# Blocks turned by TensorE's transpose instead of an fp32 matmul with the identity, in two stages of a fused convolution, attention and expert kernel

## The chip, the cores and the metric

The kernel runs as one program on one core of a Trainium2 chip. Its time is the device time of one execution in microseconds (us). The kernel before takes 1914.7 us, the median of three runs (1913.49 to 1919.65).

## What is computed

The input is x, 128 images of 256 channels and 9 x 9 pixels, in fp32. Cut to what bears on the change:

```
xn  = layernorm of x over the channels                      # per image and pixel
k1  = 9-tap convolution of xn along the channels, one filter for each of the 81 pixels, + bias
v   = 3x3 depthwise convolution of xn (one filter per channel) + bias
k1s = relu(batchnorm(3x3 depthwise convolution of xn))
out1, out2 = two attentions made of xn, k1, v and k1s
x   = x + alpha * out1 + (1 - alpha) * out2
t   = x as 10368 tokens of 256 channels
t   = t + mixture of 8 experts (two chosen per token) of layernorm(t)
```

The two stages in which the change lies make k1 ("the pixel convolution") and then v and k1s ("the depthwise convolutions").

## The kernel before, in words

The core's engines run five instruction streams that are tied by semaphores. The order on each engine is written out by hand.

**Pixel stage.** 81 pixels are taken in 27 turns of three. ScalarE normalises the three pixels of a turn out of `big` into `xp_s` (L1207; image on the partitions, 256 channels along the row). TensorE turns each of the six 128 x 128 blocks, so that channels lie on the partitions (`turn_pixels`, L408, to PSUM). ScalarE copies the turned blocks to `xt_s` (L1214). TensorE convolves them with banded matrices, two fp32 matmuls of 132 columns per pixel (`convolve_pixels`, L419 and L421). VectorE adds the bias and writes k1 to `pool_` (L770), and it copies the normalised pixels back to `big` (L763). Everything is double-buffered, and TensorE turns the blocks of turn i+1 ahead of the convolution of turn i.

**Depthwise stage.** 256 channels go in 8 chunks of 32, and each chunk in 8 quads of four channels. A chunk begins with the turning of its first quad. Then TensorE makes the chunk's convolution matrices, nine times nine small bf16 matmuls (L457), which ScalarE (L1242, five times) and VectorE (L820, four times) copy to `m_s`; the PSUM banks for it are two pairs, so each group of nine matmuls waits for the copy two groups back. Then come the quads. For each, GpSimd copies four channels of xn (L1397), TensorE turns the four 128 x 81 blocks (`turn_quad`, L441), VectorE copies the result to `pt_s` (L826), TensorE multiplies it with the four channels' matrices (L475, 162 columns), ScalarE copies the two results out (L1251, L1253) and SyncE stores them. TensorE's order is: turn of quad q+1, then the multiplication of quad q. Before the first multiplication of a chunk it waits for the last copy of the matrices (L1242).

TensorE's other turned blocks, those of the attention (L531), of the token rows (L592), of the expert rows (L637) and of the end (L695), already go through `nc.tensor.transpose`.

A matmul with fp32 operands shows as two pairs of records in the trace, each a weight load (LDWEIGHTS, engine PEld) and a MATMUL (engine PE). So the 6 blocks of a pixel turn are 12 records at L408, and the 4 blocks of a quad are 8 records at L441.

Of the kernel before, what the change touches and what calls it, by code (L numbers as in the profile page):

```python
# [4 lines left out]
BS, C, H, W = 128, 256, 9, 9  # L5
HW = H * W
# [39 lines left out]
def metaformer_kernel(nc, x, taps, tap_bn, tap_rows, toeplitz_mask, ident, band_masks, rot_masks, zstrings,  # L46
# [14 lines left out]
    with ctx:  # L61
        def sb(name, shape, dt=fp32):
            return ctx.enter_context(nc.sbuf_tensor(name, shape, dt))
# [15 lines left out]
        ident_s = sb("ident_s", [128, 128])  # L79
# [42 lines left out]
        def take_aux(parts, *dims, dt=fp32):  # L122
            n = 1
            for d in dims:
                n *= d
            words = n if dt != fp16 else n // 2
            a = aux[0:parts, aux_at[0]:aux_at[0] + words]
            aux_at[0] += words
            assert aux_at[0] <= AUX
            a = a if dt == fp32 else a.bitcast(dt)  # L130
            names = "abcde"[:len(dims)]
            if len(dims) > 1:
                a = a.rearrange(f"p ({' '.join(names)}) -> p {' '.join(names)}",
                                **{m: d for m, d in zip(names, dims)})
            return a
# [3 lines left out]
        xp_s = take_aux(128, 2, PIX, C)  # L139
# [3 lines left out]
        ps = ctx.enter_context(nc.psum_tensor("ps", [128, 8, 512], fp32))  # L143
# [17 lines left out]
        xq_s = take_aux(128, 2, QUAD, HW)  # L161
# [235 lines left out]
        def _(pe):  # L397
            pe.wait_ge(S["w_in"], W_IN)

            def turn_pixels(i, par):  # L400

                pe.wait_ge(S["xp_c"], i + 1)
                pe.wait_ge(S["xt_c"], i - 1 + CREDIT)
                for k in range(PIX):
                    for h in range(HALVES):
                        at = (k % 2) * C + h * 128

                        last = nc.tensor.matmul(ps[:, 2 * par + k // 2, at:at + 128], xp_s[:, par, k, h * 128:(h + 1) * 128],  # L408
                                                ident_s[:, :], start=True, stop=True)
                last.then_inc(S["tr_c"], 1)  # L410

            def convolve_pixels(i, par, come):
# [10 lines left out]
                last.then_inc(S["k1_c"], 1)  # L423

            turn_pixels(0, 0)
            with pe.Fori(0, PIX_TURNS // 2) as i:
                for par in range(2):
                    turn_pixels(i * 2 + par + 1, 1 - par)
                    convolve_pixels(i * 2 + par, par, i + 1)
# [5 lines left out]
            def turn_quad(q, par):  # L435

                pe.wait_ge(S["xq_c"], q + 1)
                pe.wait_ge(S["pt_c"], q - 1 + CREDIT)
                for c in range(QUAD):

                    last = nc.tensor.matmul(ps[0:HW, 4 + par, c * BS:(c + 1) * BS], xq_s[:, par, c, :],  # L441
                                            ident_s[:, :], start=True, stop=True)
                last.then_inc(S["tq_p"], 1)

            per_chunk = CHUNK // QUAD
            with pe.Fori(0, C // CHUNK) as i:
                turn_quad(i * per_chunk, 0)

                pe.wait_ge(S["ks_c"], i * per_chunk + CREDIT)
                pe.wait_ge(S["tapc_c"], i + 1)  # L450
                for n in range(9):
# [4 lines left out]
                    for m in range(9):  # L456
                        last = nc.tensor.matmul(flat[:, m * 2 * CHUNK:(m + 1) * 2 * CHUNK].rearrange("p (v c) -> p v c", v=2),  # L457
                                                mask_s[:, n * 9 + m, :],
                                                tapc_s[:, :, :],
                                                start=True, stop=True)  # L460
                    last.then_inc(S["mb_p"], 1)
                for k in range(per_chunk):
                    q, par = i * per_chunk + k, k % 2
                    if k + 1 < per_chunk:
                        turn_quad(q + 1, 1 - par)
                    if k == 0:
                        pe.wait_ge(S["mb_e0"], i * 5 + 5)
                        pe.wait_ge(S["mb_e1"], i * 4 + 4)
                    pe.wait_ge(S["pt_c"], q + 1 + CREDIT)
                    if k >= 2:  # L470
                        pe.wait_ge(S["ks_c"], q - 1 + CREDIT)
                    b0 = 6 if par == 0 else 2
                    for c in range(QUAD):
                        o = ps[:, b0 + c // 2, (c % 2) * 2 * HW:(c % 2 + 1) * 2 * HW]
                        last = nc.tensor.matmul(o, pt_s[:, par, c, :], m_s[:, k * QUAD + c, :, :]  # L475
                                                .rearrange("p v n -> p (v n)"), start=True, stop=True)
                    last.then_inc(S["cv_p"], 1)
# [3 lines left out]
            for h in range(HALVES):  # L481
                last = nc.tensor.matmul(ps[:, 6, 0:EXPERTS], ones_s[:, :], router_s[:, h, :], start=h == 0, stop=h == 1)
# [207 lines left out]
            with pe.Fori(0, TURNS) as g:  # L690
                pe.wait_ge(S["mix_c"], g + 1)
                pe.wait_ge(S["fin_c"], g + CREDIT)
                for h in range(HALVES):
                    for s in range(SUBS):
                        last = nc.tensor.transpose(ps[:, h, s * 128:(s + 1) * 128], mix_s[:, s, h * 128:(h + 1) * 128],  # L695
                                                   ident_s[0:128, 0:128])
# [849 lines left out]
```

## Time and profile before

| what | value |
|---|---|
| median of three runs | 1914.7 us |
| profiled execution: span from the first to the last instruction | 1986.5 us |
| TensorE matmul busy in the span | 1444.1 us (73%) |
| mean granted TensorE clock | 0.817 of full |
| pixel stage | about 67 to 151 us of the span |
| depthwise stage, TensorE | 175 to 396 us of the span |
| L408: records, busy | 324, 44.6 us |
| L441: records, busy | 512, 78.9 us |

The page gives no other time for the profiled execution than its span; the span is 71.8 us above the median of the runs. The granted clock is a share of full speed: 1.00 is 2.4 GHz and 0.50 is 1.2 GHz. "PE" is the matmul side of TensorE, "PEld" its weight loads, "DVE" VectorE, "ACT" ScalarE, "POOL" GpSimd and "SP" SyncE. Matmuls are pipelined, so the busy time of a single record (some 275 ns at full clock) is longer than the step from one record to the next (some 110 ns).

### The profile page before, as it was taken

Reading aid. Unit: us, or ns where it says so; the run is one execution under the profiler, and the core shown is the slowest. Engines: PE = TensorE matmul, PEld = TensorE weight load, DVE = VectorE, ACT = ScalarE, POOL = GpSimd, SP = SyncE. Lnnn points to the kernel's source line nnn. Section 1 sums busy time; section 2 is a strip of 40 time slices with the busy share of each in tenths; the row PEclk is TensorE's granted clock in tenths of the full one; section 3 lists DMA queues with packets and bytes.
Section 4 is the critical chain, followed back from the end, with each engine's and each line's share of the span. In section 5 each row is a group of like instructions: output and inputs, shape, how many; then the busy total and the mean of one; then the engine's idle time right before and its main releaser. Section 6 shows DMA issues by size and latency. Waiting matters only on the chain.

```text
span 1986.5 us, 37743 instructions
## 1 busy us (share of the span) xinstructions
PE 1444.1 (73%) x10088; PEld 1176.6 (59%) x10089; DVE 1129.8 (57%) x2738; ACT 733.0 (37%) x1671; POOL 523.6 (26%) x520
## 2 busy tenths in 40 slices
PE   0594888889999999985454526999999999811111
PEld 0594888846666666655343425888888888711111
DVE  6893333356667666746666665555555555434443
ACT  0692444444444344426555542333333333200000
POOL 0000111124333333314555550000000000077764
PEclk9996788889999999965555557999999999955555
DMA  8424445476766676612222233222222222246655
GB/s 285 102 72 169 173 182 187 159 189 164 171 165 156 152 182 153 158 38 94 96 94 97 96 124 109 90 84 95 85 90 90 88 91 84 69 118 140 141 126 117
DMA packets 312390, 251.93 MB, mean 127 GB/s; under 512 B 184061, under 2 KB 290894, under 8 KB 311652
## 3 DMA queue, kind: packets, MB, share of 16 engines
q1 hardware_dynamic: 292719, 198.56, 35.1%
q0 software_dynamic: 19648, 53.11, 9.6%
q8 instruction: 9, 0.15, 0.0%
q14 instruction: 14, 0.11, 0.0%
HBM read 151.84 MB, written 105.39 MB: 129 GB/s over the span
## 4 chain that ended last, share of the span: by engine, by line
PE 60%; DVE 14%; issue 9%; POOL 7%; DMA 3%; ACT 3%; another core or an unknown queue 2%; DVEq 1%; SPq 1%; ACTq 0%; POOLq 0%
PE ps L668 12%; PE ps L653 11%; POOL aux L1444 7%; PE ps L492 5%; PE ps L475 4%; PE ps L441 3%; PE ps L519 3%; PE ps L547 2%; PE ps L543 2%; ACT pool_ L1242 2%; PE ps L502 2%; PE ps L637 2%; PE ps L511 2%; PE ps L545 2%
## 5 line engine op out<-in xcount | busy, mean ns | idle before, releaser
L1444 POOL DMA_INDIRECT aux<-y_d,idx_s x162 | 172.5, 1065 | 602.8 <-issue 595.7
L668 PE MATMUL ps<-pool_,aux 128*128 x2112 | 248.6, 274 | 10.8 <-DVE aux L1128 4.4
L653 PE MATMUL ps<-aux,pool_ 128*128 128x256 f16 x2112 | 246.6, 274 | 0.4 <-DVE aux L1120 0.4
L668 PEld LDWEIGHTS ps<-pool_,aux 128*128 128x128 f16 x2112 | 199.2, 98 | 56.6 <-issue 31.5
L653 PEld LDWEIGHTS ps<-aux,pool_ 128*128 x2112 | 207.3, 98 | 24.6 <-issue 0.8
L1421 POOL DMA_INDIRECT rows_d<-aux,idx_s x162 | 157.7, 974 | 168.5 <-issue 101.0
L1134 DVE SCALAR_TENSOR_TENSOR pool_<-ps,pool_ 128x512 f32<-128x512 f32 x88 | 60.9, 692 | 243.8 <-PE ps L668 243.8
L1365 ACT ACTIVATE aux<-ps,b_s 128x256 f32<-128x256 f32 x352 | 137.8, 474 | 160.5 <-DVE aux L1128 160.5
L695 PE MATMUL ps<-ident_s,aux 128*128 128x128 f32 x162 | 41.5, 429 | 201.2 <-DVE aux L1173 139.8
L695 PEld LDWEIGHTS ps<-ident_s,aux 128*128 128x128 f32 x162 | 30.8, 221 | 211.9 <-issue 211.9
L1397 POOL COPY aux<-big 128x324 f32 x64 | 29.2, 457 | 360.9 <-PE ps L441 186.9
L492 PE MATMUL ps<-pool_,se_w_s 81*81 81x512 f32 x256 | 118.7, 607 | 5.7 <-DMA pool_<-k_d 5.7
L1413 POOL DMA_DIRECT2D pool_<-v_d x64 | 50.0, 781 | 274.2 <-PE ps L549 269.5
L1357 ACT ACTIVATE aux<-ps 128x512 f16<-128x512 f32 x88 | 52.6, 597 | 181.7 <-PE ps L637 181.7
L1128 DVE TENSOR_TENSOR aux<-aux 128x1024 f16<-128x1024 f32 x88 | 107.8, 1225 | 3.1
L1277 ACT ACTIVATE pool_<-ps,sa_ab 128x324 f32<-128x324 f32 x64 | 39.7, 620 | 159.4 <-PE ps L504 159.4
L441 PE MATMUL ps<-ident_s,aux 128*81 128x128 f32 x512 | 78.9, 305 | 25.4 <-POOL aux L1397 25.4
L610 PE MATMUL ps<-aux,before_s 128*128 128x8 f32 x54 | 16.1, 372 | 110.8 <-DVE aux L1032 89.9
L408 PE MATMUL ps<-ident_s,aux 128*128 128x128 f32 x324 | 44.6, 290 | 69.6 <-ACT aux L1207 69.6
L826 DVE COPY aux<-ps 81x512 f32<-81x512 f32 x64 | 43.9, 686 | 87.7 <-PE ps L441 87.7
L1289 ACT ACTIVATE pool_<-ps,pool_ 128x81 f32<-128x81 f32 x256 | 79.5, 336 | 29.4 <-DVE pool_ L857 29.4
L475 PE MATMUL ps<-pool_,aux 82*128 82x162 f32 x512 | 89.7, 324 | 0.0
(203 smaller groups left out, 3111.9 us busy)
## 6 DMA issues: line engine op xcount, KB each, us to landing
pool_<-rows_d SPq DMA_DIRECT2D x88, 256.0 KB, 2.7
y_d<-pool_ SPq DMA_DIRECT2D x88, 256.0 KB, 2.2
big<-in_x SPq DMA_DIRECT2D x2, 5184.0 KB, 20.8
xn_d<-big SPq DMA_DIRECT2D x16, 648.0 KB, 3.0
v_d<-aux SPq DMA_DIRECT2D x64, 162.0 KB, 1.9
ks_d<-aux SPq DMA_DIRECT2D x64, 162.0 KB, 2.0
pool_<-xn_d SPq DMA_DIRECT2D x32, 324.0 KB
pool_<-k_d SPq DMA_DIRECT2D x32, 324.0 KB
```

The costliest lines, as they stand in the source:

```text
L441: last = nc.tensor.matmul(ps[0:HW, 4 + par, c * BS:(c + 1) * BS], xq_s[:, par, c, :], ident_s[:, :], start=True, stop=True)
L475: last = nc.tensor.matmul(o, pt_s[:, par, c, :], m_s[:, k * QUAD + c, :, :] .rearrange("p v n -> p (v n)"), start=True, stop=True)
L492: last = nc.tensor.matmul(ps[0:HW, n, :], se_w1_s[:, k, :], kq_s[:, par, k, 2 * n:2 * n + 2, :].rearrange("p b j -> p (b j)"), start=k == ...
L653: last = nc.tensor.matmul(o, w_s[:, a, bass.ds(e * (4 * PIECE) + (k * HID + j * 128), 128)], xh_s[:, par, b, k * SLOTS:(k + 1) * SLOTS], s ...
L668: last = nc.tensor.matmul(ps[:, 6 + par, s * C:(s + 1) * C], hh_s[:, par, a, j, s * 128:(s + 1) * 128], w_s[:, b, bass.ds(e * (4 * PIECE) ...
L695: last = nc.tensor.transpose(ps[:, h, s * 128:(s + 1) * 128], mix_s[:, s, h * 128:(h + 1) * 128], ident_s[0:128, 0:128])
L1128: nc.vector.tensor_tensor(lo, hf_s, hi, ALU.subtract).then_inc(S["hlo_c"], 1)
L1134: nc.vector.scalar_tensor_tensor(yo_s[:, par], ps[:, 6 + par, :].rearrange("p (s c) -> p s c", s=2), 1.0 / WSCALE, b2_s[:, bass.ds(e * C, ...
L1289: ins = nc.scalar.activation(e_s[:, par, h, b, :], ps[:, 2 + h, b * HW:(b + 1) * HW], ACT.Exp, bias=sm_s[:, par, 2, j:j + 1], accum_out=sm ...
L1365: nc.scalar.activation(hf_s[:, j * SLOTS:(j + 1) * SLOTS], ps[:, 2 + 2 * par + j // 2, (j % 2) * SLOTS:(j % 2 + 1) * SLOTS], ACT.Gelu, bia ...
L1421: nc.gpsimd.indirect_dma_start(out=rows_d[:, :], out_offset=bass.IndirectOffsetOnAxis(ap=idx_s[:, slot, k:k + 1], axis=0), in_=xf_s[:, slo ...
L1444: nc.gpsimd.indirect_dma_start(out=got_s[:, par, k, :], out_offset=None, in_=y_d[:, :], in_offset=bass.IndirectOffsetOnAxis(ap=idx_s[:, pa ...
```

## The change

Both places that turn blocks call `nc.tensor.transpose` in place of `nc.tensor.matmul` with the identity as the moving operand. Source, destination, shapes and the order on every engine stay as they are, and so do all waits and all buffers. The transposed form of L531 and L637 shows as one pair of records for each block, where the fp32 matmul shows as two.

```diff
@@ turn_pixels
-                        last = nc.tensor.matmul(ps[:, 2 * par + k // 2, at:at + 128], xp_s[:, par, k, h * 128:(h + 1) * 128],
-                                                ident_s[:, :], start=True, stop=True)
+                        last = nc.tensor.transpose(ps[:, 2 * par + k // 2, at:at + 128],
+                                                   xp_s[:, par, k, h * 128:(h + 1) * 128], ident_s[:, :])
@@ turn_quad
-                    last = nc.tensor.matmul(ps[0:HW, 4 + par, c * BS:(c + 1) * BS], xq_s[:, par, c, :],
-                                            ident_s[:, :], start=True, stop=True)
+                    last = nc.tensor.transpose(ps[0:HW, 4 + par, c * BS:(c + 1) * BS], xq_s[:, par, c, :],
+                                               ident_s[:, :])
```

## Rows read from the trace of the kernel before

**Rows 1.** Page, part 2: TensorE's granted clock in 40 slices, in tenths.

```profile
PEclk9996788889999999965555557999999999955555
```

**Rows 2.** Windows of the pixel stage: us, busy of each engine (records), clock, DMA.

```profile
88.00:140.00 52.00, 51.98 (x431) 49.36 (x431) 51.20 (x55) 52.00 (x72) 0.00 (x0) 1.00 0.29 72
```

**Rows 3.** Timeline of the pixel stage: start us, us, engine, line, operation.

```profile
69.36 4.50 PE L408 MATMUL ps<-ident_s,aux 128*128 128x128 f32 x24 [69.36 <-ACT aux L1207]
72.38 0.81 ACT L1214 ACTIVATE aux<-ps 128x768 f32<-128x768 f32 x1 [0.94 <-PE ps L408]
...
101.58 1.60 PE L408 MATMUL ps<-ident_s,aux 128*128 128x128 f32 x12
```

**Rows 4.** Waits of TensorE, 175 to 394 us: us in total, times, longest.

```profile
PE ps L457 <- ACT pool_ L1242: 27.0, 32, 1.1
```

**Rows 5.** Timeline of the depthwise stage, one chunk, the second.

```profile
205.32 0.88 PE L457 MATMUL ps<-pool_ 75*82 75x64 bf16 x18
...
214.10 1.98 PE L441 MATMUL ps<-ident_s,aux 128*81 128x128 f32 x8
214.32 1.24 ACT L1242 ACTIVATE pool_<-ps 82x576 f32<-82x576 f32 x1 [0.93 <-PE ps L457]
215.87 2.44 PE L475 MATMUL ps<-pool_,aux 82*128 82x162 f32 x8
218.10 1.70 PE L441 MATMUL ps<-ident_s,aux 128*81 128x128 f32 x8
219.63 1.28 PE L475 MATMUL ps<-pool_,aux 82*128 82x162 f32 x8
...
222.74 1.04 PE L441 MATMUL ps<-ident_s,aux 128*81 128x128 f32 x8
223.61 1.28 PE L475 MATMUL ps<-pool_,aux 82*128 82x162 f32 x8
223.81 0.69 DVE L826 COPY aux<-ps 81x512 f32<-81x512 f32 x1 [1.30 <-PE ps L441]
224.73 1.04 PE L441 MATMUL ps<-ident_s,aux 128*81 128x128 f32 x8
...
231.81 1.04 PE L441 MATMUL ps<-ident_s,aux 128*81 128x128 f32 x8
```

**Rows 6.** Windows of the depthwise stage; columns as in rows 2.

```profile
209.30:219.30 10.00, 8.59 (x67) 8.25 (x67) 3.79 (x5) 4.50 (x5) 0.46 (x1) 0.50 0.05 20
219.50:236.40 16.90, 15.12 (x143) 14.68 (x141) 6.06 (x9) 7.61 (x16) 3.20 (x7) 1.00 0.69 254
```

**Rows 7.** Timeline: transposes of the attention and of the token rows.

```profile
854.87 1.04 PE L531 MATMUL ps<-ident_s,pool_ 128*128 128x128 f32 x8
858.88 0.42 PE L543 MATMUL ps<-pool_ 128*128 128x81 f32 x2 [2.96 <-issue]
891.13 2.82 PE L592 MATMUL ps<-ident_s,aux 128*128 128x128 f32 x12 [1.80 <-ACT aux L1304]
```

**Rows 8.** Windows around other changes of the clock; columns as in rows 2.

```profile
407.40:410.80 3.40, 3.40 (x5) 1.03 (x5) 0.00 (x0) 0.77 (x1) 0.07 (x1) 0.50 0.89 209
...
857.80:861.10 3.30, 2.23 (x14) 1.56 (x14) 3.09 (x10) 2.32 (x16) 0.00 (x0) 1.00 0.00 0
861.20:865.00 3.80, 3.80 (x16) 2.36 (x14) 3.59 (x9) 1.12 (x1) 0.00 (x0) 0.50 0.00 0
891.00:894.00 3.00, 2.87 (x14) 2.87 (x15) 1.09 (x3) 2.10 (x3) 0.00 (x0) 0.50 0.94 344
```

**Rows 9.** Page, part 5: the first matmuls of the attention.

```profile
L492 PE MATMUL ps<-pool_,se_w_s 81*81 81x512 f32 x256 | 118.7, 607 | 5.7 <-DMA pool_<-k_d 5.7
```

**Rows 10.** Timeline, first chunk: its first turn, the matrices, the next turn.

```profile
175.07 2.00 PE L441 MATMUL ps<-ident_s,aux 128*81 128x128 f32 x8 [25.45 <-POOL aux L1397]
176.86 1.45 PE L457 MATMUL ps<-pool_ 75*82 75x64 bf16 x18
...
186.26 1.98 PE L441 MATMUL ps<-ident_s,aux 128*81 128x128 f32 x8
```

## The prediction, written before the changed kernel ran

> **What bounds the kernel now.** I read the page's slices first. Of the stretches in which TensorE works hard, only the depthwise stage stands at 7 to 8 tenths of the clock; the pixel stage is at or near full and the token and last stages are at half [rows 1]. The windows and waits of the two changed stages come next, then the timeline of one chunk.
>
> Pixel stage: over 52 us ScalarE is busy for all 52.00 and VectorE for 51.20, at full clock [rows 2]. 431 TensorE records at 24 a turn are 18 turns, so a turn takes 2.89 us. TensorE is in it for two times 12 records; one such dozen takes 1.60 us up to its last end [rows 3], of which 0.27 is the pipeline's tail, so about 1.33 us, and with the convolution's dozen about 2.7 us. It is close behind, but ScalarE sets the pace.
>
> Depthwise stage: TensorE itself is the bound. Its only repeated wait is 27.0 us for the copies of the matrices [rows 4]. A quad at full clock takes 224.73 - 222.74 = 1.99 us: 0.87 for the turning (222.74 to 223.61) and 1.12 for the multiplication [rows 5]. The copy on VectorE (0.69) hides behind it. While the matrices are made the clock falls to half, and it stays there from 209.3 to 219.3 us; then it is full until 236.4 us [rows 6]. At half clock a turning takes 215.87 - 214.10 = 1.77 us and a multiplication 218.10 - 215.87 = 2.23 us [rows 5]. So the chunk pays half clock for the first turning, the first multiplication and most of the second turning, and then gets full clock back in the middle of unbroken fp32 matmuls.
>
> **What the change does to the instructions.** Per block one pair of records goes. Eight transposes take 1.04 us at full clock; less 0.27 for the tail of the last and over seven steps that is 0.11 us each. Twelve at half clock take 2.82 us; less 0.42 over eleven steps that is 0.22 us each [rows 7]. So four are 0.44 us at full clock in place of 0.87, and 0.88 us at half clock in place of 1.77. No order, wait or buffer changes. If nothing else moved, the only question would be what lies beside them.
>
> **The step on which all hangs: does the clock come back?** After the change, the half-clock stretch before each return consists of transposes for 0.88 us and multiplications for 2.23 us in turn. The multiplications use 82 of 128 rows, and would be 72% of the time. What rows say on such a mixture: at 407.4 to 410.8 us TensorE is busy 3.40 of 3.40 us with L492 (81 rows, 81 columns), and the clock stays at 0.50 [rows 8, 9]. A full stretch of matmuls on a part of the array is thus not enough there. Twelve transposes in a row at 891.13 us, with small matmuls behind them, 2.87 busy of 3.00 us, also leave it at 0.50 [rows 7, 8]. Twelve fp32 matmuls of the same shape at 69.36 us, with twelve more behind them, raise it: the 24 take 4.50 us [rows 3], which is some 2.9 us for the first twelve and 1.6 for the others. On the other side, after L511 and eight transposes (854.87) TensorE idles for 2.96 us and the clock is still full up to 861.1, falling only after a sparse stretch, 2.23 busy of 3.30 us [rows 7, 8]; that speaks for transposes being counted when a full clock is held. Neither settles it. I take it that transposes add nothing to what brings the clock back, and that the multiplications alone at 72% don't suffice: the mixture has fewer active columns and rows per us than the stretches at 214 to 219 us that did raise it, and no more than the solid one at 407.4 that did not. The Trainium skill says the same in "TensorE: Matmul & The Clock Gate", Part 4 (PE-mode transpose): full clock does not engage for transposes, which don't count as busy in the same way. No row here isolates that; by that rule the stage stays at half clock, and against it stands the row at 854.87.
>
> Worked out for one chunk, staying at half clock:
> - Matrices: made wholly at half clock they took 186.26 - 176.86 = 9.40 us in the first chunk [rows 10], against 214.10 - 205.32 = 8.78 us in the second [rows 5]. +0.6 us for seven chunks, +4.3 us.
> - First turning: 0.88 us, then TensorE waits for L1242, which ends at 214.32 + 1.24 = 215.56, so the multiplication starts some 1.5 us after the turning did, in place of 1.77.
> - Then eight multiplications and six turnings: 8 x 2.23 + 6 x 0.88 = 23.1 us. With the 1.5 it is 24.6 us.
> - Before: from 214.10 to the next chunk's turning at 231.81 [rows 5], 17.7 us. +6.9 us, times eight: +55.3 us.
>
> **Pixel stage and starts.** The first six blocks take 1.3 us less at half clock (12 records in 2.9 us against six transposes at 0.22), and ScalarE did wait 0.94 us for them [rows 3]: -1.5 us. But the clock then rises later, since this early stretch is transposes too. A half-clock turn is six transposes at 0.22 and 12 convolution records at about 0.22 (twice the 0.11 of full clock), 3.96 us, 1.07 more than 2.89. These matmuls fill the array and are two thirds of the time, so I take three such turns, +3.2 us, and full clock afterwards; held at full clock they are some 1.35 of 2.89 us, denser than the 2.23 of 3.30 with small matmuls after which it fell. There ScalarE's pace hides the rest: nothing is gained from 27 x 0.66 us of freed TensorE time. Depthwise start: four transposes in place of the 2.00 us at 175.07 [rows 10], -0.9 us.
>
> **Sum.** 4.3 + 55.3 - 1.5 + 3.2 - 0.9 = +60.4 us on the profiled 1986.5 us. That execution is 71.8 us above the median of the runs, a difference the page doesn't place; I carry the sum over unscaled, less 1 us for chunks in which the two multiplications at the end, back to back, bring the clock up for a moment: 1914.7 + 59 = 1974 us. Bounds of the unknown parts: the pixel stage between -1.5 us (clock as before) and +28 us (26 turns at half clock); the moments of return up to 1.5 us a chunk, -12 us. The case's own range is 1958 to 1999 us.
>
> **Rivals.**
> - *The clock comes back as before.* For it: the row at 854.87; and the stretch stays unbroken work. Against: 891.13 and 407.4. Per chunk the first turning gains 0.3 us (ScalarE's copy ends it), the second, at half clock, 0.3 more by the time that full clock returns, and five at full clock 0.43 each: 2.7 us, times eight 22 us. The first turning of a chunk gains nothing: it lies beside ScalarE's last copies. VectorE (0.69 us), ScalarE and GpSimd have room in a quad of 1.55 us, and the DMA share of 0.69 [rows 6] would near 0.9, worth at most 1 us at the end. With -1.5 and -0.9 it is -24 us: 1891 us, between 1885 and 1902. The Trainium skill, "Perfetto Trace Analysis", Transposes, advises transposes in place of matmuls for turning; by that rule this case holds, and here it would be 1891 us.
> - *It comes back, but a stretch later or in some chunks only.* For it: multiplications at 72% are not sparse. A return 3 us later than at 219.4 us costs half of that, 1.5 of the 2.7 us, so some -12 us with the two starts; in half of the chunks only, +15 us: 1903 to 1930 us.
> - *The change does not do what it says:* a transpose that fills 81 of 128 columns still shows as two pairs of records. No row has this shape. Then the time is that of before, 1914.7 us.
>
> **How the numbers follow.** Half clock kept 0.56; clock as before 0.31; later or partly 0.10 (half of it faster, a quarter within, a quarter slower); no change in the records 0.03. A measurement here tells a change from none at about 0.3%, 5.7 us. Faster 0.31 + 0.05 = 0.36, within 0.3% 0.03 + 0.02 = 0.05, slower 0.59. The predicted time is the likeliest case's, 1974 us. Both signs hold much of the chance, so the range that holds 8 in 10 goes from 1886 to 1986 us; it leaves out the pixel stage wholly at half clock and the lower edge of the faster case.
>
> **What the profile after would show.** Right: L408 with 162 and L441 with 256 records; the depthwise stage's slices at 5 tenths, its quads 3.1 us apart, L475 records at their half-clock duration throughout, the attention starting some 60 us later; everything from there on as long as before. Wrong: a clock of 1.00 in the second half of each chunk and quads 1.55 us apart, with 1891 us; or two pairs for each block.

## The result: 1940.4 us, slower by 1.4%, and the profile after

| | before | after |
|---|---|---|
| median of four runs | 1917.2 us (1913.5 to 1920.0) | 1940.4 us (1934.7 to 1954.4) |
| ratio | | 1.014, 95% interval 1.010 to 1.018 |
| span of the profiled execution | 1986.5 us | 1939.9 us |
| start of the first chunk's turning | 175.07 us | 174.37 us |
| start of the attention (L492) | 405.40 us | 430.27 us |

The kernel is 23 us slower by the medians. The profiled executions show the loss in one stage: the attention starts 24.9 us later. (The two spans can't be subtracted: the profiled execution of before has a surplus behind that point. From its first token transpose (L592) to its first expert one (L637) it takes 1206.6 - 891.1 = 315.5 us, the one of after 1166.8 - 915.7 = 251.1.) The forecast was 1974 us; the direction came, at 40% of the size.

The page of the kernel after, its clock in 40 slices and three groups of part 5:

```profile
PEclk9995665659999999996555559999999999955555
L475 PE MATMUL ps<-pool_,aux 82*128 82x162 f32 x512 | 127.6, 420 | 4.5 <-ACT pool_ L1242 4.5
L492 PE MATMUL ps<-pool_,se_w_s 81*81 81x512 f32 x256 | 118.7, 607 | 5.6 <-DMA pool_<-k_d 5.6
L408 PE MATMUL ps<-ident_s,aux 128*128 128x128 f32 x162 | 25.2, 296 | 83.3 <-ACT aux L1207 83.3
```

The slices of the depthwise stage fall from 7 and 8 tenths [rows 1] to 5 and 6. L408 has 162 records, one pair for a block, so the change does what it says. L475 wasn't touched, and its records grew from 89.7 us in all (324 ns each) to 127.6 (420): the same work at a slower clock.

**The pixel stage**, timeline of TensorE (start, duration, engine, line), to be held against [rows 3]:

```profile
69.81 1.51 PE L408 MATMUL ps<-ident_s,aux 128*128 128x128 f32 x6 [69.81 <-ACT aux L1207]
71.95 1.54 PE L408 MATMUL ps<-ident_s,aux 128*128 128x128 f32 x6 [0.63 <-ACT aux L1207]
73.28 0.65 PE L419 MATMUL ps<-aux 128*128 128x132 f32 x2
...
75.92 1.25 PE L408 MATMUL ps<-ident_s,aux 128*128 128x128 f32 x6
77.01 0.39 PE L419 MATMUL ps<-aux 128*128 128x132 f32 x2
...
90.51 0.87 PE L408 MATMUL ps<-ident_s,aux 128*128 128x128 f32 x6 [0.58 <-ACT aux L1207]
...
93.38 0.87 PE L408 MATMUL ps<-ident_s,aux 128*128 128x128 f32 x6 [0.49 <-ACT aux L1207]
```

The clock rises at 76.8 us (L419's records go from 0.65 to 0.39 us a pair), some 4 us later than before. After that a turn still takes 93.38 - 90.51 = 2.87 us, ScalarE's pace; TensorE now waits 0.5 us in it, and nothing comes of its freed time.

**The depthwise stage.** First the first chunk, in which the clock comes back in the middle; then the fifth, in which it doesn't (TensorE's timeline, as [rows 5]):

```profile
184.70 1.12 PE L441 MATMUL ps<-ident_s,aux 128*81 128x128 f32 x4
186.38 2.52 PE L475 MATMUL ps<-pool_,aux 82*128 82x162 f32 x8 [0.56 <-ACT pool_ L1242]
188.70 1.06 PE L441 MATMUL ps<-ident_s,aux 128*81 128x128 f32 x4
189.55 2.37 PE L475 MATMUL ps<-pool_,aux 82*128 82x162 f32 x8
191.71 1.06 PE L441 MATMUL ps<-ident_s,aux 128*81 128x128 f32 x4
192.57 1.42 PE L475 MATMUL ps<-pool_,aux 82*128 82x162 f32 x8
193.82 0.60 PE L441 MATMUL ps<-ident_s,aux 128*81 128x128 f32 x4
194.26 1.28 PE L475 MATMUL ps<-pool_,aux 82*128 82x162 f32 x8
195.37 0.60 PE L441 MATMUL ps<-ident_s,aux 128*81 128x128 f32 x4
```

```profile
302.38 2.52 PE L475 MATMUL ps<-pool_,aux 82*128 82x162 f32 x8 [0.56 <-ACT pool_ L1242]
304.69 1.06 PE L441 MATMUL ps<-ident_s,aux 128*81 128x128 f32 x4
305.55 2.37 PE L475 MATMUL ps<-pool_,aux 82*128 82x162 f32 x8
...
319.76 1.06 PE L441 MATMUL ps<-ident_s,aux 128*81 128x128 f32 x4
320.61 4.53 PE L475 MATMUL ps<-pool_,aux 82*128 82x162 f32 x16
324.93 1.06 PE L441 MATMUL ps<-ident_s,aux 128*81 128x128 f32 x4
```

The quads are 1.55 us apart (195.37 - 193.82) where the clock is full, and 3.01 us (191.71 - 188.70) where it is half. Windows of the second to fifth chunk (us, busy of PE, PEld, DVE, ACT, POOL, then clock, DMA share and GB/s), against [rows 6]:

```profile
212.50:230.30 17.80, 17.80 (x71) 17.74 (x72) 3.53 (x6) 4.07 (x11) 2.36 (x6) 0.50 0.40 148
230.50:237.10 6.60, 4.66 (x58) 4.21 (x56) 2.35 (x4) 3.84 (x8) 0.91 (x2) 1.00 0.61 226
237.30:250.80 13.50, 11.14 (x74) 10.48 (x75) 5.05 (x6) 5.62 (x8) 0.91 (x2) 0.50 0.15 55
251.00:264.40 13.40, 10.87 (x112) 10.42 (x111) 5.80 (x8) 7.11 (x14) 2.74 (x6) 1.00 0.78 287
302.40:326.00 23.60, 23.59 (x92) 23.15 (x92) 4.35 (x8) 6.17 (x16) 2.86 (x7) 0.50 0.39 141
```

TensorE is busy all the time in 212.5 to 230.3 and in 302.4 to 326.0, and still at half clock. In the second chunk the clock comes back at 230.4, when only the last multiplications are left, and is spent on the next chunk's matrices, which wait for their copies anyway. Lengths of the first seven chunks, from the start of one first turning to the next, and returns of the clock in the eight chunks:

| kernel | chunk lengths, us | clock full in the middle / only at the end / never |
|---|---|---|
| before | 29.2 27.6 27.4 27.4 27.4 27.3 27.3 | 8 / 0 / 0 |
| after | 26.8 31.6 26.4 31.6 34.1 26.7 34.1 | 3 / 2 / 3 |

These counts, like those of every run below, are of the one profiled execution. The four runs of the kernel after go from 1934.7 to 1954.4 us, three times the spread of before, with a mean granted clock of 0.804 to 0.792, so other executions can have other counts.

By chunks: the three with a mid return save 2.4, 1.1 and 0.6 us; the two late ones cost 4.1 and 4.2; the two of the never kind cost 6.8 each, and the eighth, up to L492, 7.8. That is 25.6 us, and with the start 0.7 us earlier it is the 24.9 of the table. In the profiled executions the stage accounts for the whole change.

### The profile page after: what moved, and what is told of

It is laid out like the page before. It is cut to its first block, busy times and chain, and to the rows that moved or that the text cites. A ratio compares the mean times of both kernels' runs of the same rounds, so it can differ in the third digit from the quotient of the medians.

```text
span 1939.9 us, 36907 instructions
## 1 busy us (share of the span) xinstructions
PE 1447.9 (75%) x9670; PEld 1176.1 (61%) x9671; DVE 1129.0 (58%) x2738; ACT 732.3 (38%) x1671; POOL 528.3 (27%) x520
## 4 chain that ended last, share of the span: by engine, by line
PE 61%; DVE 12%; POOL 8%; issue 8%; ACT 5%; DMA 3%; SPq 1%; DVEq 1%; ACTq 0%; POOLq 0%
PE ps L668 13%; PE ps L653 11%; POOL aux L1444 8%; PE ps L475 6%; PE ps L492 6%; PE ps L519 3%; ACT pool_ L1242 3%; PE ps L547 3%; PE ps L543 2%; PE ps L502 2%; ACT aux L1207 2%; PE ps L441 2%; PE ps L637 2%; PE ps L511 2%; PE ps L545 2%
## 5 line engine op out<-in xcount | busy, mean ns | idle before, releaser
L695 PE MATMUL ps<-ident_s,aux 128*128 128x128 f32 x162 | 41.5, 430 | 193.8 <-DVE aux L1173 193.8
L1397 POOL COPY aux<-big 128x324 f32 x64 | 29.2, 457 | 381.3 <-PE ps L441 208.0
L475 PE MATMUL ps<-pool_,aux 82*128 82x162 f32 x512 | 127.6, 420 | 4.5 <-ACT pool_ L1242 4.5
L492 PE MATMUL ps<-pool_,se_w_s 81*81 81x512 f32 x256 | 118.7, 607 | 5.6 <-DMA pool_<-k_d 5.6
L475 PEld LDWEIGHTS ps<-pool_,aux 82*128 82x128 f32 x512 | 116.1, 287 | 7.4 <-issue 7.4
L408 PE MATMUL ps<-ident_s,aux 128*128 128x128 f32 x162 | 25.2, 296 | 83.3 <-ACT aux L1207 83.3
L847 DVE TENSOR_REDUCE pool_<-ps 128x4 f32<-128x324 f32 x64 | 31.6, 495 | 92.8 <-PE ps L511 91.2
```

The source lines that it names most:

```text
L492: last = nc.tensor.matmul(ps[0:HW, n, :], se_w1_s[:, k, :], kq_s[:, par, k, 2 * n:2 * n + 2, :].rearrange("p b j -> p (b j)"), start=k == ...
```

## The experiments

Two theories at first. **U**: transposes aren't counted in what brings the clock back, and the multiplications alone don't always suffice. **R**: a transpose counts like a matmul of its shape, but takes half the time, so the half-clock stretch now holds less work that fills the rows of the array and more that uses 82 of 128. Each run is timed against the kernel before on the same chip. "Only the quads" below means that the pixel turns stay matmuls.

**Each half alone.** e1: `transpose` in `turn_pixels` only. e2: in `turn_quad` only.

> Only the pixel stage's blocks go through the transpose, the quads' stay fp32 matmuls. Both theories: the clock rises some 4 us later than in the kernel before (76.8 in place of 72.7 us, as in the changed kernel), ScalarE's pace hides everything after, and the time is that of before within 3 us (1914 to 1920 us). Had the pixel stage a part in the loss, it would be above 1925 us.

> Only the quads' blocks go through the transpose. Both theories: all of the loss is here, 1935 to 1950 us, with the clock full in some chunks and not in others, since 0.88 us of turning per 2.16 us of multiplication at half clock lies at the edge of what raises it.

e1: 1911.1 us against 1915.9, ratio 0.998 (0.996 to 1.000). e2: 1948.2 us, ratio 1.016 (1.012 to 1.019); clock back in the middle of chunks 1, 4 and 7 only. The quads are the loss. The pixel half is worth a few us at most, on the side of a gain: e1 came out 3 us under the range expected, and the four profiled executions with pixel transposes (after, e1, e4, e5) begin the first chunk at 174.2 to 174.4 us, the ten without at 175.1 to 177.3.

**Each quad transpose issued twice** (e3):

```diff
+                    for again in range(2):
+                        last = nc.tensor.transpose(ps[0:HW, 4 + par, ...], xq_s[:, par, c, :], ident_s[:, :])
```

> Each quad's transposes are issued twice, to the same place, so TensorE is busy with turning exactly as long as with the fp32 matmuls; the pixel stage is as before. Theory U (transposes are not counted in what raises the clock): the clock never comes back in a chunk, quads of 2.23 + 1.77 us, some 12.5 us more per chunk, about 2015 us. Theory R (a transpose counts like a matmul of its shape; what fell is the share of time in which all 128 rows are in use, since the multiplications use 82): the clock comes back in all eight chunks at the same place as before, 1914 to 1921 us.

1915.9 us, ratio 1.000 (0.998 to 1.001), and the clock comes back in all eight chunks. Its timeline and windows in the second chunk:

```profile
213.33 1.97 PE L442 MATMUL ps<-ident_s,aux 128*81 128x128 f32 x8
215.10 2.41 PE L476 MATMUL ps<-pool_,aux 82*128 82x162 f32 x8
217.34 1.04 PE L442 MATMUL ps<-ident_s,aux 128*81 128x128 f32 x8
```

```profile
207.50:217.00 9.50, 7.25 (x60) 6.91 (x61) 4.89 (x5) 4.52 (x4) 0.46 (x1) 0.50 0.16 62
217.50:234.00 16.50, 15.38 (x145) 15.04 (x143) 5.45 (x8) 7.41 (x17) 3.20 (x7) 1.00 0.64 235
```

Eight transposes take the time of eight records of before (1.97 against 1.98 in [rows 5]) and raise the clock as those did. Against e2, which has three returns, nothing but transposes was added. U falls.

**Fillers in the gaps.** While the matrices are made TensorE waits for copies. e4 is the changed kernel with one fp32 matmul of 448 columns behind every second group of matrices, into a PSUM bank that is free at that time and that nobody reads; e5 puts seven transposes there; e8 puts e4's matmul into the kernel before.

```diff
                     last.then_inc(S["mb_p"], 1)
+                    if n % 2 == 1:
+                        nc.tensor.matmul(ps[:, 7, 0:448], ident_s[:, :], big[:, 0:448], start=True, stop=True)
```

> Changed kernel, and after each second group of the small bf16 matmuls of a chunk's matrices one extra fp32 matmul (identity by 448 columns of xn, into a free PSUM bank, never read; 0.75 us at full clock) in the time in which TensorE waits for ScalarE. Both theories: the clock stays full through the matrices and so through the whole chunk after it has once risen; a chunk takes some 22 us in place of 27.3, about 1880 us. If the clock is not what costs the time, it stays at 1940 us or above.

> As e4, but the filling is seven transposes of 128 x 128 blocks of xn in place of the fp32 matmul: as long at full clock (0.77 us), no arithmetic. Theory R (transposes count): they hold the clock as well as the matmul did, 1870 to 1885 us. Theory U (they don't count): the clock falls while the matrices are made, the filling then takes 1.5 us in gaps of 0.7 us, and the time is above that of the changed kernel, 1950 to 1970 us.

> Kernel before with e4's filling: all turnings stay fp32 matmuls. Both theories: the clock stays full; a chunk takes e4's 22.4 us and six turnings 0.43 us longer, 24.9 us in place of 27.3, 19 us less than before: 1890 to 1902 us. With e4 it prices the transposes alone once the clock is held: some 20 us.

e4: 1876.3 us, ratio 0.981 (0.976 to 0.986), the lowest median. e5: 1883.9 us, ratio 0.982 (0.979 to 0.985). e8: 1895.8 us, ratio 0.989 (0.987 to 0.992). A stretch of e4's timeline, its window over nearly the whole stage, and e5's:

```profile
219.64 0.60 PE L441 MATMUL ps<-ident_s,aux 128*81 128x128 f32 x4
220.74 0.89 PE L457 MATMUL ps<-pool_ 75*82 75x64 bf16 x18 [0.50 <-ACT aux L1255]
221.46 1.00 PE L463 MATMUL ps<-big,ident_s 128*128 128x448 f32 x2
222.70 0.89 PE L457 MATMUL ps<-pool_ 75*82 75x64 bf16 x18 [0.24 <-ACT pool_ L1244]
...
230.37 1.37 PE L477 MATMUL ps<-pool_,aux 82*128 82x162 f32 x8 [1.03 <-ACT pool_ L1244]
...
242.00 0.60 PE L441 MATMUL ps<-ident_s,aux 128*81 128x128 f32 x4
```

```profile
178.00:355.00 177.00, 158.97 (x1457) 133.01 (x1455) 81.87 (x104) 98.08 (x167) 27.93 (x61) 1.00 0.54 200
```

```profile
186.00:346.00 160.00, 142.07 (x1458) 132.10 (x1457) 74.42 (x94) 88.54 (x148) 26.05 (x57) 1.00 0.55 203
```

The filler (L463) stands where TensorE waited, and from 177.9 us to the end of the stage's work the clock doesn't fall: a chunk is 242.00 - 219.64 = 22.4 us. With transposes for fillers (e5) it is full from 185.7 to 346.1 us, through six whole chunks, where without fillers it never stays full for more than 17.1 us in this stage; that is the second sign against U. But in e5 it does fall once, in the eighth chunk, behind its fillers and the wait for the last copy, and is half until 352.9 us:

```profile
343.37 0.65 PE L441 MATMUL ps<-ident_s,aux 128*81 128x128 f32 x4
345.05 1.54 PE L479 MATMUL ps<-pool_,aux 82*128 82x162 f32 x8 [1.03 <-ACT pool_ L1246]
346.38 1.06 PE L441 MATMUL ps<-ident_s,aux 128*81 128x128 f32 x4
```

Whether transposes hold the clock as well as matmuls do is therefore not shown; that they help to hold it is. Where the clock is held, the change is a gain: the medians of e8 and e4 are 19.5 us apart, on two chips, and by the ratios to the kernel before it is 16 us.

**Taller multiplications.** e6 is "only the quads" with the multiplications padded from 82 to 128 rows, which costs TensorE no time (2.52 us for the first eight records of a chunk at half clock, as in the kernel after). Only `pt_s` is cleared to zero there; the added rows of `m_s` hold what lay there, and count for nothing in the result. The instructions that clear and fill the buffers are left out of the cut; e7 leaves the turns of quads 2 and 3 of each chunk as fp32 matmuls.

```diff
-        m_s = take(HW + 1, CHUNK, 2, HW)
+        m_s = take(128, CHUNK, 2, HW)
...
-        pt_s = take_aux(HW + 1, 2, QUAD, BS)
+        pt_s = take_aux(128, 2, QUAD, BS)
```

```diff
-                        turn_quad(q + 1, 1 - par)
+                        turn_quad(q + 1, 1 - par, mul=k < 2)
```

> Quads by transpose, pixel stage as before, and the quads' multiplications padded from 82 to 128 rows with zeros in the moved blocks (same columns, so the same TensorE time per matmul at either clock). Theory R: with all rows in use the clock comes back in every chunk at the first chance, chunks of 23.5 to 25 us, 1885 to 1900 us, against 1948 us unpadded. If the rows in use have no part in it, it stays at 1940 to 1955 us.

> Pixel stage as before; in each chunk the two turnings that run at half clock (second and third quad's) stay fp32 matmuls, the other six are transposes. Both theories: the mixture before the clock's return is that of before, so it returns in all eight chunks, and five turnings at full clock save 0.43 us each: 17 us and up to 10 more by a shift of the moments of return, 1888 to 1900 us. If the transposes after the return made the clock fall again, it is above 1920 us.

e6: 1905.7 us, ratio 0.994 (0.992 to 0.996), clock back in all eight chunks, a little above the range expected. e7: 1897.2 us, ratio 0.989 (0.987 to 0.991), all eight. Either way of putting back what the change had thinned brings back the clock, and with the clock back the kernel is faster than before.

**Columns, rows, and a control.** e9 widens each quad transpose from 81 to 128 columns. e10 and e11 pad the multiplications to 96 and 90 rows. e12 has e10's buffers and its extra clearing, but multiplies 82 rows. The cuts of e11 and e12 are shown against e10.

```diff
-                    last = nc.tensor.transpose(ps[0:HW, 4 + par, c * BS:(c + 1) * BS], xq_s[:, par, c, :],
+                    last = nc.tensor.transpose(ps[:, 4 + par, c * BS:(c + 1) * BS], xq_s[:, par, c * HW:c * HW + 128],
```

```diff
-        m_s = take(96, CHUNK, 2, HW)
+        m_s = take(90, CHUNK, 2, HW)
```

```diff
-                        last = nc.tensor.matmul(o, pt_s[:, par, c, :], m_s[:, k * QUAD + c, :, :]
+                        last = nc.tensor.matmul(o, pt_s[0:HW + 1, par, c, :], m_s[0:HW + 1, k * QUAD + c, :, :]
```

> Only the quads' turns are transposes (the pixel turns stay matmuls, as in the run of that alone), and each of these transposes takes in and puts out 128 columns in place of 81, at the same number of rows; the extra columns are filled from padding and read by nobody. The results are as before. Theory R (what fell is the share of time in which all 128 rows of the array are in use; the width in use does not matter): as the run with the quads alone, 1940 to 1955 us, clock back in few chunks. Rival, by area (rows times columns in use): 128x128 turns weigh 1.6 times as much as 128x81 turns, and the clock comes back in all eight chunks, near 1905 us. If a wider transpose takes longer on TensorE, that is a third thing, seen in the mean of its group.

> Only the quads' turns are transposes, and each multiplication of a quad is padded from 82 rows to 96 with zeros (in the run with 128 rows it was padded to the full height, and the clock came back in all eight chunks at 1906 us). The results are as before. If each row in use counts, the mean height over a quad rises by about half of the 0.11 of the array that 14 more rows are in 96% of multiplication time: part of the way to the run with 128 rows, clock back in more chunks than three, 1905 to 1930 us. If rows count in groups of 32 (82 rows already fill three of the four), nothing changes: 1940 to 1955 us, clock back in few chunks. If only the full height counts, nothing changes either.

> As the run with 96 rows, but each multiplication of a quad uses 90 rows, which is no multiple of 32. Results as before. With 96 and with 128 rows the time was 1906 us and the clock came back in all eight chunks; with 82 it was 1948. Theory G (rows count in whole groups of 32: 82 rows weigh like 64, 96 like 96): 90 rows weigh like 64 too, 1940 to 1955 us, clock back in a few chunks. Rival, every row counts, and the border lies between 82 and 96: 90 rows are in between, and the clock comes back in most or all chunks, 1905 to 1925 us.

> Control of the runs with 96 and 128 rows: the buffers are as tall as in the run with 96 rows and VectorE clears them in the same extra instruction, but each multiplication uses 82 rows as before. Results as before. If the rows in use are what brought the clock back: 1940 to 1955 us, as with the quads alone. If the placement of the buffers or the extra clearing did it: near 1906 us.

| run | time, ratio (interval) | lengths of the first seven chunks, us | middle / end / never |
|---|---|---|---|
| e9, 128 columns | 1939.5, 1.012 (1.007 to 1.017) | 34.6 26.9 31.6 26.3 31.6 26.4 31.6 | 3 / 3 / 2 |
| e10, 96 rows | 1905.7, 0.994 (0.992 to 0.995) | 26.3 24.9 26.1 25.0 26.1 25.0 26.2 | 8 / 0 / 0 |
| e11, 90 rows | 1904.8, 0.994 (0.992 to 0.996) | 25.8 26.3 25.0 26.3 25.0 26.2 25.0 | 8 / 0 / 0 |
| e12, 82 rows, padded buffers | 1942.9, 1.012 (1.010 to 1.014) | 34.6 34.8 26.8 34.0 34.8 26.8 34.0 | 2 / 0 / 6 |

The same row of part 5 on the pages of e11 and then of e12, and a chunk of e11 around the clock's return:

```profile
L475 PE MATMUL ps<-pool_,aux 90*128 90x162 f32 x512 | 96.9, 342 | 4.5 <-ACT pool_ L1243 4.5
```

```profile
L475 PE MATMUL ps<-pool_,aux 82*128 82x162 f32 x512 | 138.1, 447 | 4.5 <-ACT pool_ L1243 4.5
```

```profile
216.04 1.06 PE L441 MATMUL ps<-ident_s,aux 128*81 128x128 f32 x4
216.89 2.37 PE L475 MATMUL ps<-pool_,aux 90*128 90x162 f32 x8
219.05 1.06 PE L441 MATMUL ps<-ident_s,aux 128*81 128x128 f32 x4
219.91 1.36 PE L475 MATMUL ps<-pool_,aux 90*128 90x162 f32 x8
221.10 0.60 PE L441 MATMUL ps<-ident_s,aux 128*81 128x128 f32 x4
```

At half clock a multiplication takes 2.37 us with 82 rows as with 90; eight more rows change nothing in the order of the instructions or in their duration at a given clock, and the clock comes back in eight chunks of eight in place of two or three. Wider transposes don't do that: e9's clock comes back in the middle of three chunks only, as in the kernel after, and its time is 1.2% above the kernel before. e10 and e11 also correct R as I first put it (only the full height of 128 counts): 90 and 96 do as well as 128. What is shown is that the rows in use of the multiplications make the difference, not only in whole groups of 32, and that the columns of the transposes don't. The same runs speak against the area in use (rows times columns): e9 adds more of it than e11 does, and only e11 brings the clock back. The columns of the multiplications weren't varied, nor whether zeros in the added rows count as other values would. With 82 rows the same sequence sometimes does and sometimes doesn't bring the clock back.

## Why the prediction was wrong

**Right.** The records (one pair for a block), the pixel stage's pace, what hides in it, and what bounds both stages. The question on which all hangs was the right one: the stage's time is decided by whether the clock comes back. The price of a chunk at half clock was right too: +6.9 us forecast for turnings and multiplications, 6.8 measured (34.1 against 27.3). In it a quad took 3.01 us and not 3.11: only the first multiplication of a chunk takes 2.3 us up to the next turning, the others 2.16, and I had counted all at 2.23. The +0.6 for matrices made wholly at half clock is 34.8 - 34.0 = 0.8 where a chunk without return follows another (e12), and doesn't occur where it follows one with a return.

**The step that failed** is "I take it that transposes add nothing to what brings the clock back, and that the multiplications alone at 72% don't suffice". The first half is false: e3 adds nothing but transposes to e2 and has eight returns of eight, and e5 keeps the clock full with them through six chunks. The second half, the multiplications alone, no run tests, because the transposes beside them count. What was drawn from both, that the clock stays half in every chunk, isn't what happened: it came back in five of eight chunks, three of them in time. That the direction came right is partly luck, since the forecast rested on transposes counting for nothing. So the term "times eight" was too large: three chunks paid 7.1 us on average, two paid 4.2, three gained 1.4, in place of eight that pay 6.9. "Later, or in some chunks only" was the case that came; I gave it 0.10, and priced it at 1903 to 1930 us. It had no case in which the clock comes back when a chunk is nearly over: that costs 4.2 us, not the 1.5 less gain of a return 3 us late. A return in the middle was put at a gain of 2.7 us if it comes where it came before, and at 1.2 if it comes 3 us later. Measured is 1.4 on average, and these returns were later: 18.4, 18.1 and 18.1 us behind the start of their chunks, against 17.0, 15.0 and 14.7 in the kernel before. With the clock full throughout the gain is 25.0 - 22.4 = 2.6 us for each chunk (e8 to e4), but that is another sum, six turnings of 0.43 us.

**How I read the rows.** The solid stretch of L492 in [rows 8] was my witness that work on a part of the array doesn't bring the clock back. It was a window cut out of a longer stretch. The whole of it, in the trace of the kernel before:

```profile
405.40:413.90 8.50, 8.50 (x11) 3.26 (x12) 0.00 (x0) 1.55 (x2) 2.99 (x2) 0.50 1.02 229
```

```profile
414.00:414.50 0.50, 0.50 (x3) 0.35 (x2) 0.00 (x0) 0.06 (x1) 0.38 (x1) 1.00 0.80 168
```

It begins after 5.12 us of idling and ends with the rise at 414.0, with two more lines' matmuls of 128 rows behind L492. Of 3.4 us inside it no more can be said than that the clock had not come back yet.

What the witness said was nearer the truth than the row could show. The fourteen profiled executions all have this stretch, L492 for 6.9 us without a gap at half clock, and in none does the clock rise in it; it rises 1.3 to 4.5 us after the first matmul of 128 rows behind it. The longest is e4's:

```profile
364.49 7.12 PE L494 MATMUL ps<-pool_,se_w_s 81*81 81x512 f32 x8 [5.81 <-DMA pool_<-k_d]
371.40 1.29 PE L504 MATMUL ps<-pool_,sa_w_s 128*128 128x324 f32 x2
```

```profile
364.50:375.80 11.30, 11.30 (x18) 5.01 (x18) 0.00 (x0) 2.17 (x3) 3.46 (x2) 0.50 1.03 222
```

L492 differs from those behind it in columns too (81 of 128), so it fits what e11 and e12 show of rows, but doesn't show it by itself. The twelve transposes at 891.13 [rows 7] had the flaw of a short window too: 3.0 us in which it had not risen. The row at 854.87, after which the clock was still full, was the one that bore on transposes, and I set it aside.

The Trainium skill, "TensorE: Matmul & The Clock Gate", Part 4 (PE-mode transpose), says that full clock doesn't engage for transposes and that they don't count as busy the same way. The runs disagree: eight returns of eight with nothing added to e2 but transposes (e3), and 160 us at 1.00 with transposes in the gaps (e5). I let that page tip a balance that the rows had left open.

**The pixel terms.** Forecast -1.5 and +3.2 us up to the first chunk; measured -0.7. (For the first the working has 1.3 us and the sum 1.5.) The clock stayed half for some two turns, not three, and most of it lay beside ScalarE, so the late rise hid better than assumed. The -0.9 in the first chunk was right: its matrices begin 175.31 - 174.37 = 0.94 us after its start, against 1.79 [rows 10].

**What stays open.** Why, with 82 rows, one chunk gets its clock back at once, one late and one never, in the same execution, with the same instructions at the same spacing. And by what measure rows enter: there are runs at 82, 90, 96 and 128 only. How the returns differ from execution to execution isn't known either, with one trace for each kernel.

## What to carry to other kernels

Where TensorE bounds a stage and its clock rises and falls in it, removing records from the stretch before a rise is not a saving of their time: ask what the rest of the stretch looks like to the clock, and test it with work put back at no cost, as padded rows or repeated transposes. Padded rows in the multiplications turned the loss into -0.6%, and two turnings of each chunk left as matmuls into -1.1%. The better remedy is in the gaps: four fillers in each chunk's waits turned +1.4% into -1.9%, where the fillers alone gave -1.1% (e8). And a short window in which a clock hasn't changed is no evidence of what doesn't change it; take the stretch from its start to the next change.

## What the runs showed of the hardware

- Transposes count in what raises TensorE's clock: e3, eight returns of eight against e2's three. They help to hold it: e5, full from 185.7 to 346.1 us, though it fell once after that.
- Unbroken busy TensorE can stay at half clock: 23.59 of 23.60 us busy at 0.50 (302.4 to 326.0 us of the kernel after), with 82 rows in most of the work; and 6.9 us of matmuls on 81 rows and 81 columns, in fourteen executions of fourteen.
- Eight more rows in a matmul of 82, zeros on one side, took no time (2.37 us for eight records at half clock either way) and moved the kernel by 38 us (e11 against e12).
- A transpose of 128 columns in place of 81 costs nothing either: 1.06 us for four at half clock both ways (e9 and the kernel after).
